# Casting the expert weights with up to four transfers in flight instead of one

## The reference

```python
xn = layernorm(x)                      # x: 4 x 4096 x 1024
x  = x + attn(xn) + ffn(xn)

# attn: k = exp(10i * (xn @ Wk)), v = xn @ Wv; two running sums over time of
# v * binder, each multiplied by its probe; scaled by 1/sqrt(t), gated, @ Wo
# ffn:
probs = softmax(xn @ gate_w)           # 8 experts
expert_idx = argmax(probs); expert_w = probs[expert_idx]
for e in range(8):
    h = gelu(xn @ w1[e] + b1[e])       # 1024 -> 4096
    y = h @ w2[e] + b2[e]              # 4096 -> 1024
    out += where(expert_idx == e, expert_w, 0) * y
```

## Time and profile before

| | |
|---|---|
| timed runs | 5800.2 and 6096.1 us, median 5948.15 us |
| the profiled execution | 5805.03 us, span of its slowest core 5803.5 us |
| spans of the eight cores | 5748.6 to 5803.5 us |
| mean granted TensorE clock | 0.918 to 0.921 of full speed |
| PE busy | 4150.2 us (72%) |
| ACT, DVE, POOL busy | 30%, 25%, 7% |
| software queue, hardware queue | 409.01 and 397.69 MB, 32.5% and 21.0% of the 16 engines' span |

### The profile page before, as it was taken

How to read it: one execution, slowest core, us unless ns; L and a number is a source line. 1 busy time by engine, 2 the same in 40 slices (tenths; PEclk the granted TensorE clock), 3 DMA queues, 4 the chain that set the end, 5 groups by cost and what they waited for, 6 DMA issues and landing times.

```text
span 5803.5 us, 52131 instructions; the slowest of 8 cores (5748.6 to 5803.5 us)
## 1 busy us (share of the span) xinstructions
PE 4150.2 (72%) x18224; PEld 1848.1 (32%) x18224; DVE 1429.7 (25%) x2651; ACT 1747.2 (30%) x2240; POOL 432.0 (7%) x727
## 2 busy tenths in 40 slices
PE   1122487788777678787887778877788778977782
PEld 0022233333333233333333333333333333333331
DVE  2233122212221222122213321122311323023231
ACT  1011233333332433332333332233323333223330
POOL 1000000000000000000010000010000100010000
PEclk9999998999888889998999999988999889989896
DMA  5876665445456445465465646575545655563333
GB/s 79 126 116 101 151 155 133 131 134 148 125 147 166 121 124 160 135 161 119 137 167 142 151 137 167 155 167 141 149 131 145 148 138 160 163 152 134 131 115 121
DMA packets 371631, 810.02 MB, mean 140 GB/s; under 512 B 71080, under 2 KB 246440, under 8 KB 337584
## 3 DMA queue, kind: packets, MB, share of 16 engines
q0 software_dynamic: 226624, 409.01, 32.5%
q1 hardware_dynamic: 144752, 397.69, 21.0%
HBM read 930.36 MB, written 157.29 MB: 187 GB/s over the span
## 4 chain that ended last, share of the span: by engine, by line
PE 54%; ACT 16%; DMA 13%; DVE 10%; issue 5%; DVEq 1%; SPq 0%; ACTq 0%; POOLq 0%
PE f_y L970 27%; PE f_h L909 20%; ACT L112 7%; DMA w1ring<-w1c 5%; DMA w2c<-w 5%; ACT f_h L112 2%; DMA ln_x<-xfh 2%; PE a_kv L628 2%; PE a_kv L623 2%; DVE accf L112 2%; DVE ln_stg L112 1%; ACT a_bnt L112 1%; ACT a_bnp L112 1%; DMA o_x<-xown 1%; PE ln_tr L404 1%
## 5 line engine op out<-in xcount | busy, mean ns | idle before, releaser
L909 PE MATMUL f_h<-f_xn,w1ring 128*128 128x512 bf16 x8192 | 1962.5, 398 | 914.2 <-ACT f_h L112 764.3
L970 PE MATMUL f_y<-f_w,f_h 128*128 128x512 bf16 x8192 | 1789.9, 381 | 91.4 <-DVE accf L112 51.9
L112 ACT ACT_TABLE_LOAD x432 | 554.3, 1283 | 3064.4 <-PE f_h L909 1522.3
L909 PEld LDWEIGHTS f_h<-f_xn,w1ring 128*128 128x128 bf16 x8192 | 811.8, 102 | 2052.0 <-issue 1235.4
L970 PEld LDWEIGHTS f_y<-f_w,f_h 128*128 128x128 bf16 x8192 | 802.5, 98 | 1072.8 <-issue 119.0
L112 ACT ACTIVATE f_h<-f_h,b_s 128x512 bf16<-128x512 f32 x1024 | 703.5, 687 | 759.5 <-PE f_h L909 732.9
L112 DVE SCALAR_TENSOR_TENSOR accf<-f_y,se_tm,accf 128x512 bf16<-128x512 f32 x224 | 168.2, 751 | 1344.6 <-PE f_y L970 1324.1
L836 POOL DMA_DIRECT2D f_w<-w2c x512 | 273.4, 579 | 2690.9 <-PE f_y L970 2630.4
L112 DVE TENSOR_SCALAR a_tA<-a_bnp 128x512 f32<-128x512 f32 x64 | 27.3, 427 | 1612.0 <-ACT a_bnt L112 1612.0
L112 DVE TENSOR_TENSOR_SCAN a_cb<-a_p,carries,consts 128x512 f32<-128x512 f32 x256 | 328.6, 1284 | 27.6 <-DVE a_p L112 1.4
L404 PE MATMUL ln_tr<-ident_s,ln_xn 128*128 128x128 f32 x256 | 62.1, 424 | 355.8 <-DVE ln_xn L112 355.8
(11 more groups left out here) (69 smaller groups left out, 1428.1 us busy)
## 6 DMA issues: line engine op xcount, KB each, us to landing
f_w<-w2c POOLq DMA_DIRECT2D x512, 512.0 KB, 5.6
w1ring<-w1c SPq DMA_DIRECT2D x256, 1024.0 KB, 6.8
w1c<-w POOLq DMA_DIRECT2D x64, 1024.0 KB, 12.2
w2c<-w POOLq DMA_DIRECT2D x128, 512.0 KB, 7.2
f_xn<-xnscr SPq DMA_DIRECT2D x32, 1024.0 KB, 8.8
a_wk<-wkc SPq DMA_DIRECT2D x64, 256.0 KB, 6.8
a_wv<-wvc SPq DMA_DIRECT2D x64, 256.0 KB, 7.1
ln_x<-xfh SPq DMA_DIRECT2D x16, 512.0 KB, 5.3
```

What stands on the lines that cost most here:

```text
L112: ins = fn(*a, **k)
L909: ins = t.matmul(hps[ctg % NHPS][:, 0:FCH], w1ring[:, slot * KT * W1CO + kt * W1CO + ct * P: slot * KT * W1CO + kt * W1CO + (ct + 1) * P], ...
L970: ins = t.matmul(yps[tt][:, 0:MMW], hsb[:, kc * FCH + tt * P: kc * FCH + (tt + 1) * P], w2ring[:, slot * KCG * MMW + k2 * MMW: slot * KCG ...
```

## The change

A piece of W1 or W2 no longer takes the semaphore of its expert but the next of the four in turn (`cast_rr`), and waits only for what was counted on that one, which is the piece four before it. Up to four pieces can be in flight. The pieces of Wk, Wv and Wo keep their single semaphore. Since an expert's last piece no longer tells that the others have landed, `tok_cast_w1[e]` and `tok_cast_w2[e]` become tuples of the tokens of all four semaphores as they stand when the last piece is issued, and `need` takes such tuples.

```diff
--- before.py
+++ after.py
@@ -70,6 +70,10 @@
 
     def need(self, eng, tok):
         if tok is None:
+            return
+        if isinstance(tok[0], (tuple, list)):
+            for t in tok:
+                self.need(eng, t)
             return
         trk, val = tok
         if val is None or val <= 0:
@@ -236,6 +240,10 @@
                 for _kcg in range(NKCG):
                     cast_pieces.append(("w2", _e, _hh, _kcg))
         cast_idx = [0]
+        cast_rr = [0]
+
+        def all_cast_toks():
+            return tuple(D["gcw%d" % k].tok for k in range(4))
 
         def emit_cast_pieces(k):
             if cast_idx[0] >= len(cast_pieces):
@@ -250,8 +258,11 @@
                     cast_idx[0] += 1
                     if pc[0] in ("kv", "wo"):
                         wg.need(g, D["gcast"].tok)
+                        sem = D["gcast"]
                     else:
-                        wg.need(g, D["gcw%d" % (pc[1] % 4)].tok)
+                        sem = D["gcw%d" % (cast_rr[0] % 4)]
+                        cast_rr[0] += 1
+                        wg.need(g, sem.tok)
                     if pc[0] == "kv":
                         j = pc[1]
                         D["gcast"].inc(g.dma_start(
@@ -274,18 +285,16 @@
                             tok_cast_kv = tok
                     elif pc[0] == "w1":
                         _e, cob = pc[1], pc[2]
-                        sem = D["gcw%d" % (_e % 4)]
-                        tok = sem.inc(g.dma_start(
+                        sem.inc(g.dma_start(
                             bass.AP(w1c, (_e * NCOB + cob) * P * KT * W1CO,
                                     [[KT * W1CO, P], [W1CO, KT], [1, W1CO]]),
                             bass.AP(w1, _e * DM * DFF + cob * W1CO,
                                     [[DFF, P], [DFF * P, KT], [1, W1CO]])))
                         if cob == NCOB - 1:
-                            tok_cast_w1[_e] = tok
+                            tok_cast_w1[_e] = all_cast_toks()
                     else:
                         _e, hh, kcg = pc[1], pc[2], pc[3]
-                        sem = D["gcw%d" % (_e % 4)]
-                        tok = sem.inc(g.dma_start(
+                        sem.inc(g.dma_start(
                             bass.AP(w2c,
                                     ((_e * NH + hh) * NKCG + kcg) * P * KCG * MMW,
                                     [[KCG * MMW, P], [MMW, KCG], [1, MMW]]),
@@ -293,7 +302,7 @@
                                     + hh * MMW,
                                     [[DM, P], [DM * P, KCG], [1, MMW]])))
                         if hh == NH - 1 and kcg == NKCG - 1:
-                            tok_cast_w2[_e] = tok
+                            tok_cast_w2[_e] = all_cast_toks()
 
         def finish_casts():
             emit_cast_pieces(len(cast_pieces))
```

## The result

Over 42 runs of the changed kernel and 41 of the kernel before, the ratio of the times is 1.0052, with a 95% interval of 1.0031 to 1.0073: the change costs half a per cent, some 30 us, and by the 2% line it is no change. The medians of all runs are 5929.27 us after and 5846.8 us before; the ratios leave out the executions in which half of the chip ran at a lower granted clock, and any that is over 1.5% above the fastest of its kernel. The profiled execution took 5854.0 us, with a span of 5852.5 us on its slowest core, core 4. A repetition on another chip gave 1.0054 (1.0017 to 1.0091).

What follows compares the result with a forecast made beforehand. It took the kernel for a matmul kernel with holes, PE's largest in the expert part being waits for gelu on ACT. Terms: 5805 - 38 + 50 + 6 + 10 + 10 - 5 = 5838 us; range 5740 to 5975.

Steps and rivals of the forecast that it cites:

- the 2% that the text gave 0.81: Chance given to a time within 2% (116 us) of the kernel before; faster got 0.07, slower 0.12.
- (d): LayerNorm: W1 casts run closer together, meeting four loads as now; W2 casts come in pairs at loads; +10 us.
- (a): Ahead of experts 5 to 7: four casts in flight fill the DMA engines, so PE's W2 waits shrink; -38 us.
- the ring at half of its full price: Upper end of the range, 5975 us, which also holds a median of one run near 5805 and one higher.
- (b): Expert stage: W1 ring loads slow down beside W2 casts in fours, in 24 new crowded stretches; +50 us.
- (c): Ring loads beside W1 casts: deeper casts lengthen the loads and shorten the stretch; +10 us.
- +6 of clock: Longer PE waits for the ring lower the clock for the matmuls that follow; a few such, +6 us.
- my fourth rival: Slower: the ring pays in full, 8.7 us in each of 24 stretches; 5805 + 232 = 6037 us, chance 0.13.
- a sign of being wrong: LayerNorm longer by more than 30 us would show the forecast wrong.
- (e): End of LayerNorm: the last W1 cast starts earlier, so PE's wait at the first ring load shrinks; -5 us.
- the second: Rival of no depth: the software queue finishes one cast before starting another, nothing changes; 5805 us, chance 0.09.
- the first, a conserved cost: Rival: the ring loses as much in fewer stretches, so (b) and its clock are 0; 5782 us, chance 0.23.

Runs made afterwards that it cites:

- experiment 1: The changed kernel, but with one cast at a time in LayerNorm and up to four in flight in the expert stage; ratio to before 1.0175.
- experiment 3: The changed kernel, but SP issues the next tile's load ahead of this tile's store; ratio to before 1.0207.
- experiment 4: The changed kernel, but with LayerNorm's tile loads issued one tile ahead; ratio to before 1.0017.
- experiment 5: The kernel of experiment 1 (single casts in LayerNorm, up to four in the expert stage), unedited, on another chip; ratio to before 1.0118.
- experiment 6: The kernel of experiment 1, but with at most two casts in flight in the expert stage; ratio to before 1.0113.

## Why the prediction was right and wrong

As a change against the profiled execution the forecast was +33 us, 0.6%, and +0.5% was measured, inside the 2% that the text gave 0.81. As a time it was not: 5838 us is below the median of the runs shown (5948.15) and reads as a fall, while the measured median is 5929.27 and the kernel got slower.

Two steps failed. The first is the choice to stand the sum beside the lower of two runs and to give that as the time; of 41 runs of before the median is 5846.8, 42 us above the execution that I summed on. The second, and the one of the mechanism, is term (d): LayerNorm at +10 us, because the W1 casts would run closer together and meet four loads "as now". It is +36, and behind it stands the premise of (a) that a busy share under one is room: in LayerNorm the share went from 0.87 to 0.99 and the eight W1 casts took 111 us instead of 105.

The range, 5740 to 5975, held the time, and that is luck too. Its upper end is said to be the ring at half of its full price, but that comes to 5805 - 23 + 255 / 2 = 5910 us, below the measured 5929.27; only the room left for a median of mixed runs reached it.

The sum of +33 came near the measured +30 by luck: the mean of the cores has -27 for W2, +26 for the ring and +36 for LayerNorm, where the text had -38, +66 and +10.

- (a) The W2 wait, -38: right. The block took 78.3 us, not 82.1, and the waits went entirely: 39.5 us on core 5, where I had counted 32.8, and 27 on the mean of the cores. The Trainium skill ("DMA: Bandwidth & Descriptors", anatomy of one DMA on the SWDGE path) has a fixed cost of about 2.0 us a DMA, by which twelve save 24 us, an estimate; they saved 24.3, and my own reading gave 20.5. Since the engines' share rose to 0.98 as well, the number does not tell the two readings apart, and by the fixed cost the eight W1 casts of LayerNorm would have gained too, which they did not.
- (b) and (c) The ring, +60 with +6 of clock: the mechanism was right, the size not. Ring waits rose by 26 us on the mean of the cores (and by 53 and 37 on cores 4 and 5, the longest of the profiled execution). Loads beside W2 casts went from 6.5 to 12.0 us, beyond my 9.7. What failed is that I gave a crowded stretch one price. It goes from about 2 us a chunk for pairs far apart to 8 for pairs in step. The changed kernel's profiled pairs were mostly apart; the pairs in step of experiments 1, 3 and 4, whose expert stretch is 60 to 125 us longer than the 4981 of before, go some way to my fourth rival but not to its 232 us.
- (d) LayerNorm, +10: it is +36 on the mean and +50 on core 5, past the 30 us that I had named as a sign of being wrong. The W1 casts met three loads and not four, but for waits of 20 to 31 us each, since a load stands behind the store on SP's queue, and this store went from 9.7 to 21.8 us. I had looked at the load and never at the store ahead of it. The W2 pairs that I feared cost little: the four waits after these are 7.8, 7.1, 5.6 and 5.5 us.
- (e) The first ring load, -5: wrong. The wait on core 5 is 27.12 us, 28.71 before, and on the mean of the cores it grew, from 22 to 26.
- The turn-taking between queues of the Trainium skill ("DMA: Bandwidth & Descriptors", queues, rings and completion order), as I read it, made depth free for a transfer on the other queue. The runs speak against that reading: at four in flight the store takes twice what it takes beside one. The page's rule itself is about packets, and what a packet of a cast holds no trace here shows.
- The rivals: depth was there (POOL's waits), so the second is out; the first, a conserved cost, gives -28 us for the expert stretch and my sum +28; measured are -8 on the mean of the profiled cores, so it lies a little nearer, and it misses LayerNorm.

## What to carry over

When one queue is given more depth, look at every short transfer on the other queue, and at what stands behind it in program order; here the price was paid there. A busy share of 0.80 to 0.87 of the DMA engines left 24 us to win in one place and nothing in the other. Place background transfers in the part of the loop where the foreground needs none, and spread them evenly, before trying more in flight: here place and spread gave 1.7%, and a load issued one tile ahead about as much again, with one cast at a time. Compare cores in pairs before judging a variant, and in the executions that have no profile too, because the slowest pair sets the time.

## What I had not expected of the hardware

The ring waits of a core go with the lag to its neighbour: 7.7 us a chunk when the two cores of a pair run within 4 us of each other with deep casts, 2.1 when they are 24 us or more apart. And the deep casts in LayerNorm may in part have been a help: in the profiles of the changed kernel the pairs left it 10 to 15 us apart, with single casts there and deep ones behind (experiments 1, 5 and 6) 1 to 9, and of the latter more fell into step. That may be why undoing the harm in LayerNorm alone (experiment 1) cost 1.2 to 1.8% in all instead of 0.5%; it was not tested by itself.
